# Splitting the first expert weights inside the attention loop, and fetching the second weights by three transfers

## What is computed

```python
x = _layernorm(x + attention(x, Wq, Wk, Wv, Wo, bo))
logits = softmax(q[..., :, None] * k[..., None, :]) @ v     # q, k, v = split(x @ wqkv.T), 8 columns each
top_logits, idx = top_k(logits, 2)
scores = softmax(top_logits)
for e in range(8):
    a, g = split(x_rep @ w1[e].T, 2)                        # w1: (8, 704, 128)
    he = silu(a) * g @ w2[e].T                              # w2: (8, 128, 352)
    out += where(expert_ids == e, he, 0)
x = _layernorm(x + (out * scores).sum over the two choices)
```

## Time and profile before

| What | Value |
|---|---|
| median of 3 executions | 832.68 us |
| the profiled execution | 833.07 us |
| its span in the trace | 831.3 us |
| PE, ACT, POOL, DVE busy | 91%, 85%, 78%, 64% of the span |
| mean granted TensorE clock | 0.979 of full speed |
| end of the attention block in the trace | about 687.5 us |

### The profile page before, as it was taken

How to read it: one execution, slowest core, us unless ns; L and a number is a source line. 1 busy time by engine, 2 the same in 40 slices (tenths; PEclk the granted TensorE clock), 3 DMA queues, 4 the chain that set the end, 5 groups by cost and what they waited for, 6 DMA issues and landing times. The chain is left out here.

```text
span 831.3 us, 22282 instructions
## 1 busy us (share of the span) xinstructions
PE 759.1 (91%) x9183; PEld 521.9 (63%) x9183; DVE 531.4 (64%) x829; ACT 707.3 (85%) x946; POOL 652.5 (78%) x416
## 2 busy tenths in 40 slices
PE   1899999999999999999999999999999884899991
PEld 0346566656565656566666566666665564898990
DVE  6857666666666666667686667676765767643453
ACT  3899998989898999999999989998989896766672
POOL 5789887878787878788899879999999963267641
PEclk9999999999999999999999999999999996999996
DMA  5602138303030303030304040404120005013312
GB/s 180 155 2 51 31 82 149 78 5 77 5 77 5 77 5 78 5 78 5 81 2 115 2 117 2 115 14 104 31 56 8 21 27 132 26 40 98 104 42 89
DMA packets 43139, 49.31 MB, mean 59 GB/s; under 512 B 6785, under 2 KB 27655, under 8 KB 42912
## 3 DMA queue, kind: packets, MB, share of 16 engines
q1 hardware_dynamic: 39872, 43.31, 21.2%
q0 software_dynamic: 2496, 4.24, 1.6%
q10 hardware_dynamic: 672, 0.33, 0.2%
HBM read 14.28 MB, written 9.25 MB: 28 GB/s over the span
## 5 line engine op out<-in xcount | busy, mean ns | idle before, releaser
L887 POOL TENSOR_TENSOR pl<-p,ph 128x1024 f16<-128x1024 f32 x242 | 511.5, 2130 | 71.8 <-ACT ph L789 71.6
L950 DVE TENSOR_REDUCE mx<-mps 128x1 f32<-128x1024 f32 x249 | 303.9, 1221 | 132.1 <-PE mps L621 129.8
L788 ACT ACTIVATE p<-sps,escale 128x1024 f32<-128x1024 f32 x256 | 286.4, 1119 | 47.5 <-PE sps L601 39.8
L789 ACT ACTIVATE ph<-sps,escale 128x1024 f16<-128x1024 f32 x256 | 285.2, 1114 | 0.0
L699 PE MATMUL pair_bank<-v,ph 128*128 128x65 f16 x2048 | 214.5, 193 | 6.7 <-DVE ao L990 4.3
L699 PEld LDWEIGHTS pair_bank<-v,ph 128*128 128x128 f16 x2048 | 190.7, 96 | 42.4 <-POOL pl L887 7.1
L701 PE MATMUL pair_bank<-v,ph 128*128 128x64 f16 x2048 | 214.4, 195 | 0.0
L703 PE MATMUL pair_bank<-v,pl 128*128 128x65 f16 x2048 | 213.9, 192 | 0.0
L701 PEld LDWEIGHTS pair_bank<-v,ph 128*128 128x128 f16 x2048 | 190.0, 97 | 28.4
L600 PE MATMUL sps<-q_hh,k_hl 128*128 128x512 f16 x512 | 194.9, 381 | 2.2 <-ACT ph L789 1.9
L601 PE MATMUL sps<-q_lm,k_h 65*128 65x512 f16 x512 | 195.4, 382 | 0.0
(11 more groups left out here) (257 smaller groups left out, 972.0 us busy)
## 6 DMA issues: line engine op xcount, KB each, us to landing
q_hh<-hi SPq DMA_DIRECT2D x60, 128.0 KB, 2.3
q_lm<-lo SPq DMA_DIRECT2D x30, 128.0 KB, 2.4
k_h<-hi SPq DMA_DIRECT2D x30, 128.0 KB, 2.5
k_hl<-hi SPq DMA_DIRECT2D x29, 128.0 KB, 2.5
k_hl<-lo SPq DMA_DIRECT2D x29, 128.0 KB, 2.6
sorted<-pad SPq DMA_DIRECT2D x1, 2990.0 KB, 17.6
xb<-sorted SPq DMA_DIRECT2D x46, 65.0 KB, 2.0
v<-in_w1T SPq DMA_DIRECT2D x8, 352.0 KB, 3.6
```

The lines of the kernel that those rows point to most:

```text
L788: nc.scalar.activation(p32[:, n % 4, :], sps[:, n % 2, :], ACT.Exp, bias=EXP_BIAS, scale=escale[:, 0:1])
L789: nc.scalar.activation(ph[:, n % 4, :], sps[:, n % 2, :], ACT.Exp, bias=EXP_BIAS, scale=escale[:, 0:1]).then_inc(s_exp, 1)
L887: nc.gpsimd.tensor_tensor(pl[:, n % 4, :], p32[:, n % 4, :], ph[:, n % 4, :], ALU.subtract).then_inc(s_subp, 1)
L950: nc.vector.tensor_reduce(mx[:, i // TB, i % TB:i % TB + 1], src, AX.X, ALU.max).then_inc(s_mx, 1)
```

## The change

The high parts of w1 are made by ACT inside the loop, six in pair 14 (steps 1, 4, 6, 9, 11, 14) and two in pair 15 (steps 13 and 14), after the exponentials of the step. The low parts are made by DVE in pair 15 (steps 5, 6, 7, 9, 10, 11, 14, 15), after `last_low_parts` of the step, and they overwrite w1 in place. The high parts take the memory of the projections' weights and inputs, which for that purpose become slices of one tile, `work`. The expert weights' work leaves the mixture block. w2 comes by three transfers (one for each chunk of F, all experts together), issued after the fetches of blocks 0, 1 and 2 in place of ahead of all. `aoT2`, `yb` and `back` become slices of the freed memory.

```diff
+HIGH_W1_AT = {(14, 1): 0, (14, 4): 1, (14, 6): 2, (14, 9): 3, (14, 11): 4, (14, 14): 5, (15, 13): 6, (15, 14): 7}
+LOW_W1_AT = {(15, 5): 0, (15, 6): 1, (15, 7): 2, (15, 9): 3, (15, 10): 4, (15, 11): 5, (15, 14): 6, (15, 15): 7}
+WORK = 6 * H * HD + 2 * T * P + 4 * S
...
+        self.w1_lo = first_values[:, 0:end].bitcast(F32R).rearrange("p (e f) -> p e f", e=E)
+        self.w1_hi = work[:, 0:end].bitcast(F32R).rearrange("p (e f) -> p e f", e=E)
...
@@ attention, scalar, in each step
+                    if (pp, s) in HIGH_W1_AT:
+                        e = HIGH_W1_AT[pp, s]
+                        act.wait_ge(f.s_w1, 16 * E)
+                        for a in range(2):
+                            act.wait_ge(s_head[a], spreads(a, PAIRS))
+                        nc.scalar.copy(f.w1_hi[:, e, :], f.w1[:, e, :]).then_inc(f.s_w1hi, 1)
                     front_at(nc, act, "scalar", f, pp, s)
...
@@ attention, vector, in each step
                     if LAST_LOW <= n + 2 < PAIRS * PCH:
                         last_low_parts(n + 2)
+                    if (pp, s) in LOW_W1_AT:
+                        e = LOW_W1_AT[pp, s]
+                        dve.wait_ge(f.s_w1hi, e + 1)
+                        nc.vector.tensor_tensor(f.w1_lo[:, e, :], f.w1[:, e, :], f.w1_hi[:, e, :],
+                                                ALU.subtract).then_inc(f.s_w1lo, 1)
...
@@ mixture, sync
-            for e in range(E):
-                sp.dma_start(w2[:, e, 0:2, :], io["w2T"][e:e + 1, 0:2 * P, :].rearrange(
-                    "o (c p) h -> p (o c) h", p=P)).then_inc(s_w2, 16)
-                sp.dma_start(w2[0:F - 2 * P, e, 2, :], io["w2T"][e:e + 1, 2 * P:F, :].rearrange(
-                    "o p h -> (o p) h")).then_inc(s_w2, 16)
+            def fetch_second_weights():
+                for c, (off, n) in enumerate(F_CHUNKS):
+                    sp.dma_start(w2[0:n, :, c, :], io["w2T"][:, off:off + n, :].rearrange(
+                        "e p h -> p e h")).then_inc(s_w2, 16)
...
             for i in range(NBB):
                 fetch_block(i)
+                if i == 2:
+                    fetch_second_weights()
...
@@ mixture, tensor
-            pe.wait_ge(s_wlo, E)
-            pe.wait_ge(s_w2, 16 * 2 * E)
+            pe.wait_ge(f.s_w1lo, E)
+            pe.wait_ge(s_w2, 16 * len(F_CHUNKS))
...
@@ mixture, scalar
-            act.wait_ge(f.s_w1, 16 * E)
-            high_weights(0)
             for half in range(2):
                 act.wait_ge(s_ao, half + 1)
                 nc.scalar.activation(aoT[:, half, :], bank[:, half, :], ACT.Copy,
                                      scale=mem["vinv"][:, 0:1]).then_inc(s_aoT, 1)
-            for e in range(1, E):
-                high_weights(e)
             act.wait_ge(s_spread, 1)
...
@@ mixture, vector
-            low_weights(0)
             add_output(0)
             then(statistics_of(nc, f, range(TB, TB + 4)))
             add_output(1)
             then(statistics_of(nc, f, range(TB + 4, T)))
             spread_of(nc, f, range(TB, T)).then_inc(s_spread, 1)
-            low_weights(1)
             factors(slice(TB, T), 1)
             nc.vector.tensor_copy(f.square[:, 0:1], f.shift[:, TB:TB + 1]).then_inc(s_shifted, 1)
             apply_here(range(TB + 4, T)).then_inc(s_normed[1], 1)
-            for e in range(2, E):
-                low_weights(e)
```

More of the change, by code:

```diff
@@ L129, with __init__ @@
 class Front:
-    def __init__(self, nc, ctx, y, v):
+    def __init__(self, nc, ctx, y, v, work):
         sb = lambda name, shape, dt: ctx.enter_context(nc.sbuf_tensor(name, shape, dt))
@@ L173, in __init__ @@
         self.s_wg, self.s_w1, self.s_const, self.s_gexp = sem("s_wg"), sem("s_w1"), sem("s_const"), sem("s_gexp")
+        self.s_w1hi, self.s_w1lo = sem("s_w1hi"), sem("s_w1lo")
         self.s_chain = {"vector": sem("s_vector_chain"), "pool": sem("s_pool_chain")}
@@ L474, in attention @@
         vinv = mem["vinv"]
[L475 to L480, removed]
+        work = mem["work"]
+        w_hi = work[:, 0:3 * H * HD].rearrange("p (k c) -> p k c", k=3)
+        w_lo = work[:, 3 * H * HD:6 * H * HD].rearrange("p (k c) -> p k c", k=3)
+        xT_hi = work[:, 6 * H * HD:6 * H * HD + T * P]
+        xT_lo = work[:, 6 * H * HD + T * P:6 * H * HD + 2 * T * P]
+        hi = work[:, WORK - 4 * S:WORK - 2 * S].rearrange("p (k c) -> p k c", k=2)
+        lo = work[:, WORK - 2 * S:WORK].rearrange("p (k c) -> p k c", k=2)
         q_hh = sb("q_hh", [P, 2, 2, S], F16)
@@ L1104, in mixture @@
         f.rows.append(sb("rows1", [P, 2, TB, ROW], F32))
[L1105 to L1109, removed]
+        aoT = mem["flat"][:, T * H * VW - 2048:].bitcast(F32).rearrange("p (h c) -> p h c", h=2)
+        w1_hi, w1_lo = f.w1_hi, f.w1_lo
+        free = mem["flat"][:, TB * H * VW:].bitcast(F32)
         w2 = sb("w2", [P, E, 3, D], F32)
@@ L1116, in mixture @@
         heT = sb("heT", [P, 2, 3 * P], F32)
-        yb = sb("yb", [P, YB, D], F32)
-        back = sb("back", [P, T, 2, D], F32)
+        yb = free[:, 2 * T * D:2 * T * D + YB * D].rearrange("p (n d) -> p n d", n=YB)
+        back = free[:, 0:2 * T * D].rearrange("p (t s d) -> p t s d", t=T, s=2)
         bank = ctx.enter_context(nc.psum_tensor("bank", [P, 8, 512], F32))
@@ L1132, in mixture @@
         s_normed = [sem("s_normed_act"), sem("s_normed_dve")]
-        s_whi, s_wlo = sem("s_whi"), sem("s_wlo")
         s_xb = [sem(f"s_xb{k}") for k in range(NBB)]
@@ L1273, in _ @@
         def _(act):
-            def high_weights(e):
-                nc.scalar.copy(w1_hi[:, e, :], w1[:, e, :]).then_inc(s_whi, 1)
-            act.wait_ge(f.s_w1, 16 * E)
-            high_weights(0)
             for half in range(2):
@@ L1387, in add_output @@
                     "p (q d) -> p q d", q=4), y[:, tiles, :], ALU.add))
-            def low_weights(e):
-                dve.wait_ge(s_whi, e + 1)
-                nc.vector.tensor_tensor(w1_lo[:, e, :], w1[:, e, :], w1_hi[:, e, :], ALU.subtract).then_inc(s_wlo, 1)
             then = lambda ins: f.then(dve, "vector", ins)
@@ L1501, in bass_transformer_layer_moe @@
             "flat": sb("v", [P, T * H * VW], F16),
+            "work": sb("work", [P, WORK], F16),
             "s_ids": ctx.enter_context(nc.semaphore("s_ids")),
@@ L1504, in bass_transformer_layer_moe @@
         mem["v"] = mem["flat"][:].rearrange("p (t h c) -> p t h c", t=T, h=H)
-        mem["front"] = Front(nc, ctx, mem["y"], mem["flat"])
+        mem["front"] = Front(nc, ctx, mem["y"], mem["flat"], mem["work"])
         attention(nc, io, mem)
```

## The result

| | Before | Changed |
|---|---|---|
| median beside each other, 11 executions each | 834.02 us | 836.60 us |
| ratio | | 1.0033, 95% interval 1.0023 to 1.0044 |
| the profiled execution | 833.07 us | 836.59 us |
| its span in the trace | 831.3 us | 834.8 us |
| PE, ACT, POOL, DVE busy | 91, 85, 78, 64% | 91, 85, 77, 64% |

The change costs 0.33%: 2.8 us, where 0.7 was forecast (a ratio of 1.0008). Times differ by the day and the chip, so the ratio counts; on the forecast's median it gives 832.68 x 1.0033 = 835.4 us.

The account below looks back on a forecast made before the run. It took PE as the bound from the seam to the end, POOL in pair 14, ACT in pair 15 and the seam's chain. Loop +2.4 and seam -1.7 gave +0.7 on 832.68, 833.4 us; range 829.2 to 836.8.

Parts of the forecast that it names:

- High parts 0 to 5: Pair 14 on ACT: six high parts, 4.1 us of work, cost 0 on the path, covered by POOL's subtractions.
- The rival that they are exposed: Pair 14: the high parts are not hidden, 4.1 us on the path, total +4.8, 837.5 us; chance 0.08.
- Step 7 and 8: Pair 15: step 7's low part delays step 8's normalise by 0.82 us and makes ACT 0.73 us late.
- Step 11 and 12: Pair 15: step 11's low part delays step 12's normalise, passed on in full, +0.82 us.
- Tail: End of pair 15: low parts 6 and 7 delay DVE's last addition and last normalise, together +0.87 us.
- The seam: Between attention and expert work: root earlier on ACT, -1.45 us, DVE's first routing step faster, -0.24; sum -1.7 us.
- w2 and the fetches: SP's queue: three fetches first, then w2 by three transfers, still in time for PE; cost 0.
- After the seam: From the seam to the end PE's fixed order is the bound, so the seam's gain moves the rest as a whole.
- The pair-15 delays are not absorbed: Rival for pair 15: delays absorbed, only the tail's 0.87 counts, total -0.8, 831.9 us; chance 0.2.
- POOL is not shut out: Rival for pair 15: DVE's subtractions shut out POOL's sends, total +8.7, 841.4 us; chance 0.05.
- rival four: Seam on ACT: the table load stays behind the wait, the seam gives 0.4, total +2.0, 834.7 us; chance 0.1.
- the clock did not hold: Rival for the seam: a shorter PE stop keeps the clock up, saving about 4 us, total -3.3, 829.4 us; chance 0.12.

Follow-up runs that it names:

- run 1: Changed kernel with all eight low parts moved from pair 15 to the mixture block, high parts left in the loop: 860.38 us, 0.9977 of the kernel before.
- run 2: Changed kernel with the low parts of steps 7 and 11 moved to steps 8 and 12: 862.26 us, 1.0000 of the kernel before; again 859.81 us, 0.9984.
- run 6: Changed kernel with one low part in pair 15, in step 7, the other seven in the mixture block: 860.78 us, 1.0007 of the kernel before.
- run 3: Changed kernel with the last two low parts moved to the start of the mixture block: 863.26 us, 1.0015 of the kernel before.
- run 4: Changed kernel with four low parts in pair 15 (steps 5, 6, 9, 10), four in the mixture block: 859.76 us, 0.9975 of the kernel before; again 858.19 us, 0.9976.
- run 8: Changed kernel with w2 by sixteen transfers ahead of all fetches, as in the kernel before: 861.95 us, 1.0014 of the kernel before.
- run 7: Kernel before, profiled unchanged (1.0006 against itself), and with POOL's twelve sends of pair 15 moved to the start of the mixture block: 859.82 us, 0.9988.

## Why the prediction was right in most steps and low in one

The total of 833.4 was 2.0 us too low and inside its range, and "within 0.5%" was right. In the profiled pair 3.5 - 0.7 = 2.8 us are missing from the sum, and nearly all of them lie at two places, 1.5 us in step 8 and 1.4 behind the seam, where the granted clock was at 1.2 GHz.

- **High parts 0 to 5, cost 0.** Right: 0.06 us in the trace, and run 1 shows that they cost nothing in time. The rival that they are exposed, +4.8, is out.
- **Step 7 and 8, +0.73.** This is the step that failed, in its size. DVE and PE came at the forecast times to 0.07 us, and the sentence "their last matmul ended at 673.99 + 0.38 = 674.37, now 675.19" took those matmuls at full clock. They ran at half: +2.2, by 1.5 us more. The text looked for the clock in the seam alone, and there for a gain; PE's wait had gone from 0.86 to 1.66 us, and before the change no stop in pair 15 was longer than 1.29 us. Runs 2, 6, and 3 beside 4 agree in time, and run 3's profile in the fall itself.
- **Step 11 and 12, +0.82.** Right: 0.8. Its reason was not quite so: two exponentials were still to come behind step 12, at 681.05 and 682.05 before the change.
- **Tail, +0.87.** Right by the trace: 0.8. Not separated by run 3.
- **The seam, -1.7.** Right to 0.02 us in the profile, by its own steps: the load ran ahead of the wait, and the copies left ACT. Run 1 qualifies one of them. There POOL's first copies lie beside DVE's low parts again, and yet the routing step isn't slowed, since with five low parts in place of six and one ahead of the factors all of them are over earlier. The 0.24 seems to belong to the order of that work, not to its absence.
- **w2 and the fetches, 0.** Right: 10.36 us of issues behind 2.36, all covered; run 8.
- **After the seam, 0.** "What the seam gains moves the rest as a whole" did not hold: 0.4 us went because a half clock of the same 17.1 us reached further into the expert work, and 1.0 behind the wait at 760.96. A wait of 1.90 us in the kernel before passed at full clock, so the second may look like chance; but the mean clock of 0.975 in all eleven executions says that each had as much half clock, wherever it lay. The median ratio, 2.8 us against 3.5 in the profiled pair, leaves room for some of this in the slower executions of the kernel before, too (they lie between 831.9 and 835.5 us); that isn't shown.

*Rivals.* The pair-15 delays are not absorbed: both come through. POOL is not shut out. A send that begins early in one of DVE's subtractions lasts 1.7 to 1.8 us in place of 0.96, but it did so in the kernel before as well, and a low part right behind the subtraction doesn't make it longer. The send of 671.12 ends at 672.82, and the subtraction in which it began (670.76, 1.23 us) at 671.99, 0.8 us earlier; before the change it was the same 0.8. The owner step runs at 676.91, while DVE goes on till 691. The Trainium skill, "SBUF — State Buffer", section "Who interferes with whom", calls the shared port pair an exclusive lock. The trace agrees in that a send begun inside a subtraction lasts longer; that a queue of sends is shut out by subtractions without a pause, it doesn't show. Whether each send got in between two neighbouring ones isn't shown either. The table load does run early: rival four is out. And the clock did not hold in the seam; it fell at two places more.

What stays open is why PE's stop of 1.66 us came with a fall and the ones of 1.49 us (step 12), 1.86 us (ahead of the first transposes at 691.56) and, in the kernel before, 1.90 us did not. Run 8 has a stop of 1.59 us in step 12 at full clock, and with the sends moved (run 7) the clock fell just behind a stop of 1.10 us, which at 1.09 us passed at full clock in the profile of the forecast. So the length of a stop alone doesn't decide it, and how often the 1.4 us is paid isn't known. And one profile on these chips says little: the first transposes stand at 693.0 in the kernel before, 697.3 in run 1 and 694.3 in run 4, though 1 and 4 take the same time within 0.02%. Their verdicts rest on the timed ratios alone.

## What to carry to other kernels

An engine that is busy two thirds of the time may still stand in the loop that feeds the bound engine: put extra work behind the instruction that others wait for, not ahead of it; here one step later was worth 3.5 us of 860 (1.7 to 5.3). Ask which engine's work blocked a stretch before emptying it for all of them: moving ACT's copies brought nearly all of the 1.7 us, and moving DVE's subtractions brought nothing and cost nearly four. When a change lengthens a stop of the TensorE by 0.8 us, count the chance of some microseconds at half clock behind it.

## What the runs showed of the hardware

- A stop of PE of 1.66 us in a loop that is otherwise full was followed by 3.4 us at 1.2 GHz in one profile and by 6.8 us in another; one of 1.10 us by 3.4 us; one of 1.79 us by about 3.4 us; those of 1.49, 1.59, 1.86 and 1.90 us by none.
- The seams of the two kernels compared, 20.1 and 18.4 us long, had the same 17.1 us at half clock, so the shorter one left more of it to the work behind.
- A table load of 1.28 us ran at once after the instruction ahead of it, 4.6 us before the input of its own instruction was there. Here the load cost nothing, since ACT would have waited anyway.
- On some chips PE makes stops of up to 2.4 us for no cause that the profile shows while POOL sends rows by indirect DMA, 4.5 us in pair 15, and none there with the sends moved away (one profile of each).
- A send of POOL that began early in a subtraction of DVE with two inputs lasted 1.70 to 1.80 us in place of 0.96 and ended 0.8 us behind that subtraction, with or without another one right behind.
- The whole program takes 861 us on those chips and 834 elsewhere; the stops in pair 15 are 4.5 us of it, and what makes the rest isn't shown.
